# Turning the second normalised rows by DMA instead of on the tensor engine, in a fused cross-attention and expert kernel

## The reference

```python
# cross-attention, 32 heads of 16, context of 256 columns, rotary positions
x = x + attention(layernorm(x), ctx, pos, pos, Wq, Wkv, Wout, bout)
# one shared expert and 16 routed ones, two per row, inner size 352
h = layernorm(x)                                   # the "second normalised rows"
logits = h @ gate_w.T                              # 512 -> 16
top2 of sigmoid(logits) + bias; gating = their scores, normalised
y = swiglu(h, shared) + sum over the two chosen e of gating_e * swiglu(h, e)
x = x + y
# swiglu(h, a, b, c) = silu(h @ a.T) * (h @ b.T) @ c.T
```

## Time and profile before

| | |
|---|---|
| time, three runs | 686.03, 691.12, 695.58 us; median 691.12 |
| the profiled execution | 689.33 us, its span 687.5 us |
| granted TensorE clock | 0.984 of full speed, mean |
| stages in that span | attention to about 317 us, shared to about 420, routed to the end |

### The profile page before, as it was taken

How to read it: one execution, slowest core, us unless ns; L and a number is a source line. 1 busy time by engine, 2 the same in 40 slices (tenths; PEclk the granted TensorE clock), 3 DMA queues, 4 the chain that set the end, 5 groups by cost and what they waited for, 6 DMA issues and landing times.

```text
span 687.5 us, 19434 instructions
## 1 busy us (share of the span) xinstructions
PE 635.5 (92%) x7104; PEld 406.6 (59%) x7104; DVE 503.2 (73%) x976; ACT 368.9 (54%) x620; POOL 332.9 (48%) x390
## 2 busy tenths in 40 slices
PE   2769999999999999988999999999998999999992
PEld 1346666666666666656566566666665666666661
DVE  8779888888888888866486935776765676666671
ACT  4255655666565666566411115665664666666660
POOL 3524555555555555432000012468565478777661
PEclk9989999999999999999999999999999999999997
DMA  9824744544444445650322662665877954555942
GB/s 316 222 48 64 176 112 97 88 94 94 99 99 99 99 99 122 93 125 33 123 92 62 217 210 87 197 197 92 210 219 196 279 111 92 100 85 151 262 77 33
DMA packets 105279, 90.63 MB, mean 132 GB/s; under 512 B 71632, under 2 KB 75728, under 8 KB 105232
## 3 DMA queue, kind: packets, MB, share of 16 engines
q1 hardware_dynamic: 91600, 59.76, 33.4%
q0 software_dynamic: 8752, 20.71, 15.5%
q10 hardware_dynamic: 4880, 9.52, 4.1%
HBM read 69.85 MB, written 22.81 MB: 135 GB/s over the span
## 4 chain that ended last, share of the span: by engine, by line
PE 79%; DMA 5%; DVE 5%; issue 4%; POOL 2%; ACT 2%; SPq 2%; POOLq 0%; ACTq 0%; DVEq 0%
PE p_sc L724 14%; PE p_qk L693 13%; PE p_sc L693 12%; PE p_qk L504 8%; PE p_v L504 8%; PE p_pv L593 4%; PE p_pv L596 3%; DMA used_twice_too<-used_twice 3%; PE p_tr L687 2%; PE p_pv L711 2%; PE p_sc L552 2%; PE p_pv L603 2%; PE p_sc L573 2%; PE p_sc L576 1%; SPq L425 1%
## 5 line engine op out<-in xcount | busy, mean ns | idle before, releaser
L1085 DVE TENSOR_REDUCE negmax<-p_sc 128x4 f16<-128x512 f32 x128 | 79.4, 684 | 6.0 <-PE p_sc L552 4.6
L933 ACT CAST hiddenT<-p_pv 128x384 f16<-128x384 f32 x54 | 25.9, 479 | 107.0 <-PE p_pv L711 103.2
L811 ACT ACTIVATE prob<-p_sc 128x512 f32<-128x512 f32 x128 | 66.1, 602 | 20.2 <-PE p_sc L576 19.9
L1491 POOL DMA_INDIRECT out<-prob,to_at x38 | 69.4, 1826 | 11.1 <-issue 9.7
L724 PE MATMUL p_sc<-used_twice,hiddenT 128*128 128x512 f16 (+1 forms) x306 | 71.7, 379 | 0.9 <-DVE hiddenT L1215 0.9
L1471 POOL COPY from_at<-from_rows 128x1 uint32 (+1 forms) x40 | 33.1, 828 | 80.8 <-DVE from_rows L1330 77.4
L693 PE MATMUL p_qk<-used_twice,xeT 128*128 128x352 f16 x420 | 68.4, 313 | 0.5 <-DMA xeT<-xn2T_dram 0.5
L693 PE MATMUL p_sc<-used_twice,xeT 128*128 128x352 f16 x420 | 68.4, 312 | 0.0
L1211 DVE TENSOR_TENSOR hidden<-p_sc,act_g 128x352 f32<-128x352 f32 x55 | 28.8, 524 | 52.5 <-PE p_sc L693 32.0
L920 ACT COPY xeT<-p_tr 128x1024 f16<-128x1024 f16 x40 | 40.5, 1012 | 37.4 <-PE p_tr L687 35.8
L504 PE MATMUL p_qk<-used_twice,xnT 128*128 128x512 f16 x192 | 52.1, 399 | 6.4 <-DVE swp L1063 6.4
(11 more groups left out here) (180 smaller groups left out, 1463.6 us busy)
## 6 DMA issues: line engine op xcount, KB each, us to landing
w<-e SPq DMA_DIRECT2D x20, 1408.0 KB
w<-e SPq DMA_DIRECT2D x20, 512.0 KB
out<-stream SPq DMA_DIRECT2D x17, 256.0 KB, 2.0
xn_dram<-xn_parts SPq DMA_DIRECT2D x16, 256.0 KB, 2.2
xn2T_dram<-xn2T SPq DMA_DIRECT2D x16, 256.0 KB, 2.5
w<-e SPq DMA_DIRECT2D x20, 192.0 KB
stream<-x ACTq DMA_DIRECT2D x1, 3584.0 KB, 18.0
xeT<-xn2T_dram ACTq DMA_DIRECT2D x14, 256.0 KB, 2.7
```

What stands on the lines that cost most here:

```text
L811: act.activation(prob[:, c % RING, :], p_scored(c)[:], ACT.Exp, scale=SCALE).then_inc(exp_ready, 1)
L1085: dve.tensor_reduce(negmax[:, c % 2, at:at + CH], p_scored(c)[:].rearrange("p (h t) -> p h t", t=P), AX_X, ALU.max, negate=True).then_inc( ...
L1491: pool.indirect_dma_start(out=out, out_offset=bass.IndirectOffsetOnAxis(ap=to_at[:, par, u:u + 1], axis=0), in_=ye[:, par, u], in_offset=N ...
```

## The change

`xn2_transpose`, `xn2T_copy`, `store_xn2T` and the DRAM tensor `xn2T_dram` go. SP's step gets a fifth transposing DMA, `turn_xn2`, from `xn2_parts` straight into `xn2T`. `gate_logits` and `keep_logits` of a batch move from step b+4 to step b+5, where they stand ahead of `negmax_transpose` and of the exponentials. `negmax_transpose` now waits in every step for the logits to be kept; `xn_transpose` waits for `neg_copy` instead. The shared tiles are read from `xn2_dram` by transposing DMAs, and ACT's ones wait until all 16 transposes of SP's `turn_xn2` have landed.

```diff
@@ SP
-            def store_xn2T(b, par):
-                sp.wait_ge(xn2T_ready, b + 1)
+            def turn_xn2(b, par):
+                sp.wait_ge(xn2_lo, b + 1)
                 if later(b, 1):
-                    sp.wait_ge(xn2T_stored, b * 16)
-                sp.dma_start(xn2T_dram[bass.ds(b * P, P)], xn2T[:].rearrange("p a c t -> p (a c t)")).then_inc(xn2T_stored, 16)
+                    sp.wait_ge(gate_done, b)
+                sp.nop().then_inc(turning, 1)
+                sp.dma_start_transpose(xn2T[:].rearrange("p a c t -> p (a c) t"), xn2_parts[:, par].rearrange("p a d -> p (a d)")).then_inc(xn2T_ready, 16)
...
                 on(-2, turn_k_parts, 1)
-                on(-5, store_xn2T)
                 on(-2, turn_q_parts, 1)
+                on(-4, turn_xn2)
                 if isinstance(b, int) and b == B - 1:
-                    sp.wait_ge(xn2T_stored, 2 * 16)
+                    sp.wait_ge(xn2_stored, 3 * 16)
                     for n in range(2):
-                        sp.dma_start(xeT[:, n].rearrange("p a c t -> p (a c t)"), xn2T_dram[n * P:(n + 1) * P]).then_inc(sems.xT_loaded[n], 16)
+                        sp.dma_start_transpose(xeT[:, n].rearrange("p a c t -> p (a c) t"), xn2_dram[n * P:(n + 1) * P]).then_inc(sems.xT_loaded[n], 16)
@@ PE
             def xn_transpose(b, par):
...
-                if later(b, 4):
-                    pe.wait_ge(logits_kept, b - 3)
+                if later(b, 3):
+                    pe.wait_ge(negT_ready, b - 2)
@@ negmax_transpose
-                if isinstance(b, int) and b + 3 > B:
+                if later(b, 2):
                     pe.wait_ge(logits_kept, b - 1)
@@
-            def xn2_transpose(b, par):
...
-                for a in range(2):
-                    for c in range(KC):
-                        mm = pe.transpose(p_xT[:, a, c, :], xn2_parts[:, par, a, c * P:(c + 1) * P], ident16[:])
-                mm.then_inc(xn2T_done, 1)
             def gate_logits(b, par):
-                pe.wait_ge(xn2T_ready, b + 1)
+                pe.wait_ge(xn2T_ready, b * 16 + 16)
+                last_xn, last_neg = (min(b + n, B) if isinstance(b, int) else b + n for n in (5, 2))
+                pe.wait_ge(xnT_lo, last_xn)
+                pe.wait_ge(negT_ready, last_neg)
+                if later(b, 1):
+                    pe.wait_ge(logits_kept, b)
@@ PE's step
                 on(-1, project_k, 1)
+                on(-5, gate_logits)
                 on(-3, negmax_transpose)
...
-                on(-4, xn2_transpose)
...
-                on(-4, gate_logits)
@@ PE, behind the steps
+            gate_logits(B - 2, 0)
             for c in range(KC):
                 project_out(B - 1, 1, c)
@@ ACT
-            def xn2T_copy(b, par):
-                act.wait_ge(xn2T_done, b + 1)
...
-                act.copy(xn2T[:], p_xT).then_inc(xn2T_ready, 1)
...
                 on(-2, q_high)
+                on(-5, keep_logits)
                 on(-3, exp, 0)
...
-                on(-4, xn2T_copy)
                 on(-3, attnT_high)
-                on(-4, keep_logits)
@@ ACT, shared stage
             def load_rows(n, u):
                 act.wait_ge(sems.u_done, n - 1)
-                act.wait_ge(xn2T_stored, (n + 1) * 16)
-                act.dma_start(xeT[:, u].rearrange("p a c t -> p (a c t)"), xn2T_dram[n * P:(n + 1) * P]).then_inc(sems.xT_loaded[u], 16)
+                act.wait_ge(xn2_stored, (n + 2) * 16)
+                act.wait_ge(xn2T_ready, B * 16)
+                act.dma_start_transpose(xeT[:, u].rearrange("p a c t -> p (a c) t"), xn2_dram[n * P:(n + 1) * P]).then_inc(sems.xT_loaded[u], 16)
```

More of the change, by code:

```diff
@@ L93, in build @@
         xn2_dram = nc.dram_tensor("xn2_dram", [T, 2 * DIM], F16, kind="Internal").ap()
-        xn2T_dram = nc.dram_tensor("xn2T_dram", [T, 2 * DIM], F16, kind="Internal").ap()
         stream = sb("stream", [P, B, DIM])
@@ L257, in build @@
         wo_done = sem("wo_done"); ln2_step = sem("ln2_step"); rstd2_ready = sem("rstd2_ready")
-        xn2T_done = sem("xn2T_done"); xn2T_ready = sem("xn2T_ready")
+        xn2T_ready = sem("xn2T_ready")
         xn2_hi = sem("xn2_hi"); xn2_lo = sem("xn2_lo")
-        xn2_stored = sem("xn2_stored"); xn2T_stored = sem("xn2T_stored"); gate_done = sem("gate_done"); logits_kept = sem("logits_kept")
+        xn2_stored = sem("xn2_stored"); gate_done = sem("gate_done"); logits_kept = sem("logits_kept")
         gate_exp = sem("gate_exp"); route = sem("route"); masks_ready = sem("masks_ready")
@@ L618, in project_out, with gate_logits @@
                     mm.then_inc(wo_done, 1)
-            def xn2_transpose(b, par):
-                pe.wait_ge(xn2_lo, b + 1)
-                last_neg = B if isinstance(b, int) and b + 2 > B else b + 2
+            def gate_logits(b, par):
+                pe.wait_ge(xn2T_ready, b * 16 + 16)
+                last_xn, last_neg = (min(b + n, B) if isinstance(b, int) else b + n for n in (5, 2))
+                pe.wait_ge(xnT_lo, last_xn)
                 pe.wait_ge(negT_ready, last_neg)
@@ L626, in xn2_transpose @@
                     pe.wait_ge(logits_kept, b)
-                for a in range(2):
-                    for c in range(KC):
-                        mm = pe.transpose(p_xT[:, a, c, :], xn2_parts[:, par, a, c * P:(c + 1) * P], ident16[:])
-                mm.then_inc(xn2T_done, 1)
-            def gate_logits(b, par):
-                pe.wait_ge(xn2T_ready, b + 1)
                 if not later(b, 1):
@@ L762, in pair @@
                     down(n, u, j, par, kinds[0])
-                    if kinds[0] == "shared" and n == 0:
-                        xn2_transpose(B - 1, 1)
                     if kinds[0] == "shared":
@@ L823, in attnT_high @@
                 act.copy(attnT[:, 0], attn_rows).then_inc(attnT_hi, 1)
-            def xn2T_copy(b, par):
-                act.wait_ge(xn2T_done, b + 1)
-                if later(b, 1):
-                    act.wait_ge(gate_done, b)
-                    act.wait_ge(xn2T_stored, b * 16)
-                act.copy(xn2T[:], p_xT).then_inc(xn2T_ready, 1)
             def xn2_high(b, par):
@@ L836, in xn2_high @@
                 if later(b, 2):
-                    act.wait_ge(xn2T_done, b - 1)
+                    act.wait_ge(xn2T_ready, b * 16 - 16)
                 act.copy(xn2_parts[:, par, 0], xn2[:, par]).then_inc(xn2_hi, 1)
@@ L928, in _ @@
             pipeline(step, act, 0, B + 2, 6, (B - 6) // 2, ahead=[ctx_high, xnT_copy])
+            keep_logits(B - 2, 0)
             def hT_high(n):
@@ L976, in pair @@
                     xeT_copy(n + 2, 0)
-                if kinds[0] == "shared" and n == 0:
-                    xn2T_copy(B - 1, 1)
                 hT_high(n + 1)
```

## The result

The changed kernel takes 721.02 us (median of 6 runs, 718.92 to 722.21), the kernel before 692.13 in the same sessions: ratio 1.0408, 95% interval 1.0368 to 1.0448. The profiled execution took 720.49 us, its span 718.7 us, at a mean granted clock of 0.966.

A forecast was written before the change was run, and what follows sets the result against it. PE, busy 92% of the span, was taken as the bound; 9.8 + 3.6 + 1.2 + 2.0 = 16.6, less 0.2, gave +16.4 us on 689.33, 705.7, and 707 as the runs' median; range 698 to 721.

The forecast's parts named there:

- rival 3: Shared tiles: transposes out of DRAM are slow, say 5.2 us, each of 13 tiles waits 1.2 us; 721 us, chance 0.23.
- The sign: Whole kernel: slower, +16.4 us; chance 0.58 of slower by two per cent, 0.38 within, 0.04 faster by as much.
- Early part of the step: Attention step, gate's product and kept logits ahead of the maxima: costs 0.88 us a step, bounds 0.3 and 0.96.
- Late part: Attention step, eight transposes removed: gains 0.18 us of 0.45, as `normalise` stands in DVE's queue; bounds 0.18 and 0.45.
- Rival 1: Attention step: late part gives back all of 0.45 us, +0.43 a step; about 699 to 702 us, chance 0.20.
- The step: Attention step: 0.88 - 0.18 = +0.70 us, 14 times in steps 5 to 18, +9.8 us.
- The fifth DMA in SP's queue: SP's queue in the attention step: fifth transposing DMA costs nothing, from -0.2 to +0.2 us a step, with 4 us of cover.
- Start of the shared stage: Tile 2's load waits until batch 15's transpose has landed: +3.6 us, bounds 2.5 and 5.5.
- two landings of 3.2: Shared stage's start: 3.2 us for batch 15's transpose, then at least 3.2 for tile 2's transposing load.
- 0.66 us head start: Attention stage's end: last `project_out` comes 0.66 us earlier, as PE's transposes and ACT's 1.01 us copy go.
- Other tiles: Other shared loads: transposing loads land in 3.2 to 4.0 us, 0.1 us for each of 12 tiles, +1.2 us.
- Beside the weights: Two shared tiles loaded beside the first routed pairs' weights: landing up to 5.6 us, 2 x 1.0, +2.0 us, bounds 0 and 6.

The follow-up runs named there:

- later edits: On the changed kernel with SP's early loads: gate's product late, batch 14's product behind the last output product, spare rows' store further ahead in SP's queue; 690.6 us.
- small-packet run: The kernel before, no transposing load, turned rows laid out so that plain loads and stores of shared tiles are 1024 runs of 256 bytes; 702.48 us, ratio 1.0141.
- run 762: Not a run's label: 762 is the count of packets that one queue moved from 388 to 393 us in the small-packet run.

## Why the prediction was right or wrong

The range, 698 to 721, met the median of 721.02 only at its edge, and the sum, +16.4 us, was about half of the +31.2 between the profiled executions. That the edge was met is luck: it came from rival 3, whose mechanism the trace refutes. The sign and the three places were right. Their order was not (forecast 9.8, 3.6 and 2.0 us for the steps, the start and the tiles beside the weights; measured about 12, 7.1 and 10.5), nor were the sizes of the last two.

**Early part of the step: right.** Forecast 0.88 us from product to maxima; 0.90 measured, with the wait of 0.4 ahead of the maxima. The product moved alone cost 0.78 a step.

**Late part: right, a little low.** Forecast 0.18 for the transposes against their full 0.45, because `normalise` stands behind DVE's rotary products. Measured 0.20 with the product early and 0.29 with it late, and DVE's row has no idle time ahead of it. Rival 1 is out. PE's freed time went into the wait for the attention rows (0.24 to 0.79 us), as forecast.

**The step.** Forecast +0.70, measured +0.58 in the steady steps. By the table steps 5 to 16 lost 7.8 us and the last two 3.3 (9.0 to 12.2), 11.1 in place of 9.8, and 0.8 more follows up to tile 0. The last steps lost more than their share because the matmuls ran slowly, with the clock at 0.50 from 316 to 320 us: the first half of `project_out` took 2.74 us (316.00) where the kernel before has 1.47 (305.87). The sum had no term for the clock. That the clock was low there is shown; why is open. The missing transposes don't decide it: from 300 to 320 us the runs with the transposing loads alone and with the small packets, which have all of PE's transposes, are at 0.86 and 0.91, and the run with early loads and late product, which has none of the removed ones, at 1.00.

**The fifth DMA in SP's queue: right.** No cost of it shows in the loop of the runs with the late product.

**Start of the shared stage: mechanism right, size half.** Forecast +3.6 (2.5 to 5.5), measured +7.1. The step of the prediction that failed is the sum's two landings of 3.2 and its 0.66 us head start. The head start did not come: the last batch's parts were ready 13.2 us behind tile 0's product in both kernels (343.57 - 330.35, and 330.46 - 317.31). The landings took 3.4 and 4.3 us. The product behind the wait ran 1.75 us slower at the low clock, for which again there was no term. The wait itself is the one that the Trainium skill demands of a second queue's first transpose (DMA: Bandwidth & Descriptors, Rules for kernel authors); with one queue for all transposes it was needless, and the 6.74 us ahead of tile 2 were gone, though 3.9 us of other waits took their place until the later edits.

**Other tiles: right.** Forecast +1.2 for twelve tiles; no wait was measured at them. A transposing read of DRAM lands in 3.3 us; the cover of 3.96 suffices. Rival 3, whose 721 us is the measured number, is wrong in its cause: not each tile was late. For a lone load the Trainium skill's "as fast as regular DMAs" (Advanced Engine Details and Errata, X-Bar Transpose) is so nearer than I took it (3.3 against 2.7 us); beside the weights it is not (9.0 against 4.4).

**Beside the weights: the term that failed.** Forecast +2.0 (0 to 6), measured 10.5: waits of 5.09 and 2.44 and 3.4 us of slow matmuls behind them (3.58 for 1.95, 2.72 and 2.91 for 1.95 each), less the wait of 0.49 that was there before. I bounded the landing by 5.6 us, the slowest transposing DMA of the earlier trace rows, which is one between SBUF tiles. The load of tile 10 took 9.0. Weights in flight are the condition (no late tile where they were loaded later), and small packets are enough for the wait at tile 10 (5.00 us with the plain load of 1024 runs); the wait at tile 12 is that of the transposing load alone, and its cause is open. The plain load of before had 144 packets and was through early (4.4 us). The Trainium skill (DMA: Bandwidth & Descriptors, SWDGE vs HWDGE vs iDMA) has it that inside each DMA engine the internal queues are served round-robin and switched at packet boundaries; the packets while both queues had work agree with that (426 beside 440, 762 beside 751), the changed kernel's first 4.0 us and its last 2 us (3 beside 345, 626 beside 294) do not show it.

## What to carry to other kernels

Count a transfer's packets before it shares the DMA engines with a big load on another queue: here a load of 1024 small packets took three times as long beside one as alone (9.0 against 3.3 us), so give it that much cover or few, large packets. When work is taken off the busiest engine, look at the next engine's queue first (here a DVE product ahead of `normalise` kept back 0.25 of 0.45 us), and when a step is moved ahead of a round trip, its own round trip is added whole. Put all transposing DMAs in one queue, and issue loads when their buffer falls free, not where their old issuer happened to be.

## What was not expected of the hardware

- Two queues served by packet count, not by bytes, while both had work: from 388 to 393 us of the small-packet run 762 packets with 0.20 MB and 751 with 1.76 MB. A load on one of them can also stand for 4.0 us before its packets begin.
- After PE had waited 5 to 7 us, its next twelve matmuls took 3.58 to 3.70 us in place of 1.95, about half speed (0.50 granted where a stretch shows it alone, the lower of the clock's two levels). In the changed kernel the twelve behind them were at 1.95 to 1.99 again; in the small-packet run they still took 3.08. A wait of 5 us so cost 6.7 to 7.8.
- A transposing load from DRAM (256 KB) landed in 3.3 us, much as one between SBUF tiles (3.2), and its issue held ACT for 1.25 us against 0.33.
